# Two graph layers on one core: the turned weights and their product with the attention vectors, made ahead of the neighbour-maximum loop

## The reference, cut to what matters

```
h = relu(layernorm(x))
x = x + max over neighbours j of h[j]              # layer 0
h = relu(layernorm(x))                             # layer 1: graph attention
wh = h @ W
e[i, j] = leaky_relu((wh @ a1)[i] + (wh @ a2)[j], 0.2)
e = where(adj > 0, e, -9e15)
x = x + elu(softmax(e, axis=1) @ wh)
```

## Time and profile before

| | us |
|---|---|
| median of 3 runs | 848.89 (844.92 to 851.26) |
| profiled execution | 848.88 |
| its span, first to last instruction | 847.0 |
| busy: VectorE | 729.1 (86%) |
| busy: TensorE | 722.5 (85%) |
| busy: ScalarE | 480.6 (57%) |
| busy: GpSimd | 347.2 (41%) |
| neighbour loop, first to last ScalarE operation of it | about 19 to 512 |
| from there to the first attention weight on VectorE | 512 to 568.8 |

### The profile page before, as it was taken

How to read it: one execution, slowest core, us unless ns; L and a number is a source line. 1 busy time by engine, 2 the same in 40 slices (tenths; PEclk the granted TensorE clock), 3 DMA queues, 4 the chain that set the end, 5 groups by cost and what they waited for, 6 DMA issues and landing times.

```text
span 847.0 us, 14904 instructions
## 1 busy us (share of the span) xinstructions
PE 722.5 (85%) x5658; PEld 498.5 (59%) x5658; DVE 729.1 (86%) x1121; ACT 480.6 (57%) x594; POOL 347.2 (41%) x320
## 2 busy tenths in 40 slices
PE   1789999999999998999999983247889999999995
PEld 1345444445444444444444442137889999999995
DVE  8899889999999998999999997327479988998994
ACT  3878898888888888888888860134421100110000
POOL 0611055565655655655565666713003321330330
PEclk9999999999999999999999996568899999999998
DMA  9799677987887777877877545202124444444410
GB/s 309 250 363 364 231 250 237 323 258 249 256 259 246 235 240 240 260 250 230 244 243 257 158 144 185 53 13 73 53 100 162 162 150 147 140 149 151 162 63 14
DMA packets 64904, 166.75 MB, mean 197 GB/s; under 512 B 7424, under 2 KB 12160, under 8 KB 60736
## 3 DMA queue, kind: packets, MB, share of 16 engines
q1 hardware_dynamic: 53776, 138.75, 47.2%
q0 software_dynamic: 11056, 27.02, 13.4%
HBM read 121.70 MB, written 44.04 MB: 196 GB/s over the span
## 4 chain that ended last, share of the span: by engine, by line
PE 40%; ACT 27%; issue 16%; DVE 9%; another core or an unknown queue 4%; DMA 2%; POOL 1%; ACTq 0%; DVEq 0%; SPq 0%
PE pick_ps L684 13%; ACT edge_t L344 12%; ACT depth L353 7%; PE order_ps L684 7%; ACT first L352 6%; PE order_ps L519 5%; DVE acc L807 4%; PE key_ps L684 3%; PE flip_ps L684 3%; PE pick_ps L538 3%; DMA subset_max<-keys 1%; PE key_ps L632 1%; DVE rest L1008 1%; PE key_ps L551 1%
## 5 line engine op out<-in xcount | busy, mean ns | idle before, releaser
L316 POOL DMA_INDIRECT found<-subset_max,entry x256 | 273.6, 1069 | 240.0 <-DVE acc L807 109.1
L807 DVE TENSOR_TENSOR acc<-pick_ps,acc 128x1024 f32<-128x1024 f32 x248 | 302.5, 1220 | 26.2 <-PE pick_ps L538 15.6
L1008 DVE SCALAR_TENSOR_TENSOR rest<-depth,acc,stage 128x512 f32<-128x512 f32 x256 | 201.4, 816 | 19.0 <-PE key_ps L684 1.5
L352 ACT ACTIVATE first<-order_ps,neg 128x1024 f16<-128x1024 f32 x128 | 142.6, 1114 | 61.4 <-PE order_ps L519 37.6
L353 ACT ACTIVATE depth<-order_ps,mid 128x1024 f16<-128x1024 f32 x128 | 141.8, 1107 | 0.0
L344 ACT ACTIVATE edge_t<-flip_ps 128x1024 f16<-128x1024 uint16 x128 | 131.2, 1025 | 3.9 <-PE flip_ps L510 2.9
L684 PE MATMUL pick_ps<-keys,rest 128*128 128x129 f32 x1024 | 121.2, 280 | 10.5 <-DVE left L960 6.5
L684 PEld LDWEIGHTS pick_ps<-keys,rest 128*128 128x128 f32 x1024 | 119.6, 197 | 13.3 <-issue 7.4
L519 PE MATMUL order_ps<-edge_t,order_w 128*128 128x512 f16 x256 | 79.5, 393 | 38.5 <-ACT edge_t L344 30.6
L538 PE MATMUL pick_ps<-first,h_hi 128*128 128x512 f16 x256 | 97.6, 381 | 5.1 <-DVE acc L807 5.0
L538 PE MATMUL pick_ps<-second,h_hi 128*128 128x512 f16 x256 | 97.4, 380 | 2.0 <-DVE acc L807 1.1
(11 more groups left out here) (154 smaller groups left out, 818.9 us busy)
## 6 DMA issues: line engine op xcount, KB each, us to landing
stage<-adj SPq DMA_DIRECT2D x64, 1024.0 KB
edge_units<-edge_t SPq DMA_DIRECT2D x64, 512.0 KB
stage<-edge_units SPq DMA_DIRECT2D x32, 1024.0 KB, 4.9
subset_max<-keys POOLq DMA_DIRECT2D x12, 512.0 KB, 8.4
found<-subset_max,entry POOLq DMA_INDIRECT x256
best<-x SPq DMA_DIRECT2D x4, 512.0 KB, 6.3
subset_max<-x POOLq DMA_DIRECT2D x4, 512.0 KB, 8.8
out<-keys POOLq DMA_DIRECT2D x7, 256.0 KB, 2.8
```

Of the source, the lines that this page charges most:

```text
L316: nc.gpsimd.indirect_dma_start(found[:, n % NG, s, :], None, subset_max, bass.IndirectOffsetOnAxis(entry[:, n, s:s + 1], 0)).then_inc(gath ...
L352: nc.scalar.activation(first[:, g % 4, :], order_ps[:, :], ACT.Relu, scale=-1.0, bias=neg[:, :]).then_inc(first_ready, 1)
L807: V.tensor_tensor(acc[:, q % 2, :], pick_ps[k][:, :], acc[:, q % 2, :], ALU.max).then_inc(raised, 1)
L1008: V.scalar_tensor_tensor(out=weight[:, n % WEIGHTS, :], in0=limit[:, q % 2, :], scalar=slope[:, c:c + 1], in1=units[:, m % EDGES, k * TI:( ...
```

## The change

The turned weights, the spread vectors and their product get SBUF tiles of their own (`w_t`, `a_wide`, `wa`) instead of places carved out of `acc`, and are made before the loop. TensorE turns the weights after `rank(0)`, for which it waits for `w_in`, and multiplies after `flip(3)`. ScalarE copies after `select(0)` and after `select(2)`. GpSimd, not VectorE, spreads the vectors, ahead of its low halves. The loop's first use of `key_ps` waits for the second copy. The steps between the loops are taken out.

```diff
+        w_t = sb("w_t", [P, D], F32)
+        a_wide = sb("a_wide", [P, 2 * D], F32)
+        wa = sb("wa", [P, 2 * D], F32)
...
-        w_t, a_wide, wa = carve(D), carve(2 * D), carve(2 * D)
...
 # GpSimd, after the iotas
+                pool.wait_ge(consts_made, 1)
+                pool.wait_ge(w_in, 48)
+                nc.gpsimd.tensor_scalar(a_wide[:, D:2 * D], ones[:, :], a12[:, 0:1], None, ALU.mult).then_inc(wide_made, 1)
+                nc.gpsimd.tensor_scalar(a_wide[:, 0:D], ones[:, :], a12[:, 1:2], None, ALU.mult).then_inc(wide_made, 1)
                 pool.wait_ge(hs_ready, 4)
...
 # ScalarE
                 select(0)
+                act.wait_ge(small_put, 1)
+                nc.scalar.activation(w_t[:, :], wt_ps, ACT.Copy).then_inc(small_took, 1)
                 high(1)
                 edges(2)
                 select(1)
                 edges(3)
                 select(2)
+                act.wait_ge(small_put, 2)
+                nc.scalar.activation(wa[:, :], wa_ps, ACT.Copy).then_inc(small_took, 1)
                 high(2)
...
-                act.wait_ge(small_put, 1)
-                nc.scalar.activation(w_t[:, :], wt_ps, ACT.Copy).then_inc(small_took, 1)
-                act.wait_ge(small_put, 2)
-                nc.scalar.activation(wa[:, :], wa_ps, ACT.Copy).then_inc(small_took, 1)
                 root(0)
...
 # TensorE
                         if n >= 1:
                             pe.wait_ge(keyed, n)
+                        else:
+                            pe.wait_ge(small_took, 2)
...
                 rank(0)
+                pe.wait_ge(w_in, 48)
+                nc.tensor.transpose(wt_ps, w_sb[:, :], ident32[:, :]).then_inc(small_put, 1)
                 flip(2)
                 rank(1)
                 flip(3)
+                pe.wait_ge(small_took, 1)
+                pe.wait_ge(wide_made, 2)
+                nc.tensor.matmul(wa_ps, w_t[:, :], a_wide[:, :], start=True, stop=True).then_inc(small_put, 1)
                 rank(2)
...
                 for g in range(4):
                     rows(g)
-                pe.wait_ge(w_in, 48)
-                nc.tensor.transpose(wt_ps, w_sb[:, :], ident32[:, :]).then_inc(small_put, 1)
-                pe.wait_ge(small_took, 1)
-                pe.wait_ge(wide_made, 2)
-                nc.tensor.matmul(wa_ps, w_t[:, :], a_wide[:, :], start=True, stop=True).then_inc(small_put, 1)
                 for g in range(4, 6):
                     rows(g)
-                pe.wait_ge(small_took, 2)
...
 # VectorE
-                dve.wait_ge(w_in, 48)
-                V.tensor_scalar(a_wide[:, D:2 * D], ones[:, :], a12[:, 0:1], None, ALU.mult).then_inc(wide_made, 1)
-                V.tensor_scalar(a_wide[:, 0:D], ones[:, :], a12[:, 1:2], None, ALU.mult).then_inc(wide_made, 1)
                 dve.wait_ge(x1_in, 16)
```

## The result

The changed kernel took 851.74 us (median of 20 runs, 849.37 to 857.86), the kernel before beside it 849.03 (20 runs, 839.43 to 854.43): 1.0059 of it, interval 1.0034 to 1.0084. It is a little slower, by less than 1%, where 2.5 us of gain were forecast. The profiled execution took 850.31 us (span 848.5) against 848.88, 1.43 more.

What follows compares the result with a forecast made beforehand. ScalarE was taken to pace the neighbour loop, with late signals under GpSimd's gathers making the gaps after it. 848.9 + 2.4 (start) - 4.9 (between the loops) = 846.4 us; range 828 to 854.

Steps and rivals of the forecast that it cites:

- Start, +2.4: Kernel start: waiting for weights and vectors, plus two copies, delays ScalarE and what follows by 2.4 us; bounds 1.7 to 3.6.
- GpSimd's two products, zero: Kernel start: GpSimd's two new 128x128 products, at most 1.57 us each, end before anything needs them and cost zero.
- Root 9.9 sooner: Between the loops: ScalarE's root needs only the moments, so it starts near 530.8 to 530.9, not 540.76, 9.9 us sooner.
- I take the middle mechanism: Between the loops: signals stay about 8 us late per hand-over until about 558.7; gain 4.9 us; chance 43%.
- rival A: Between the loops: columns held until the gathers are over, whenever made, so nothing gained; 851.3 us; chance 20%.
- Rival B: Between the loops: the lateness of signals goes, gaining 22.4 us; 828.9 us; chance 27%.
- Rival C: Between the loops: late signals strike VectorE's six steps, delaying the last gather batch; 857.8 us with two strikes; chance 10%.

Runs made afterwards that it cites:

- after_direct: Changed kernel with the 24 gathers of groups 28 to 30 replaced by plain transfers, so the rows asked for are not fetched: 826.64 us, ratio 1.002.
- before_direct: Kernel before with the 24 gathers of groups 28 to 30 replaced by plain transfers, so the rows asked for are not fetched: 824.85 us, ratio 1.0004.
- after_spaced: Changed kernel, its start too, with a 128x128 GpSimd multiply behind each of the 24 gathers of groups 28 to 30: 829.10 us, ratio 0.9749.
- before_spaced: Kernel before with a 128x128 GpSimd multiply behind each of the 24 gathers of groups 28 to 30: 826.79 us, ratio 0.9722.
- w_first: Changed kernel with the loads of the weights and vectors issued ahead of the first adjacency loads: 847.77 us, ratio 0.9988.
- after_again: Changed kernel, unchanged, timed again beside the kernel before in the third group: 852.54 us, ratio 1.0089.
- root_first: Kernel before with ScalarE's root and first normalisation ahead of the two copies and TensorE's product behind the first columns, start unchanged: 848.97 us, ratio 1.0013.
- w_wait_only: Kernel before with only TensorE's wait for weights and vectors behind its first rank product added at the start: 849.76 us, ratio 1.0038.
- direct_again: Kernel before with the 24 gathers of groups 28 to 30 as plain transfers, run again in the third group: 826.86 us, ratio 0.9804.
- before_pause: Kernel before with GpSimd waiting ahead of the gathers of group 28 until the curve shifts are made: 852.29 us, ratio 1.0065.

## Why the prediction was wrong

**Start, +2.4: right.** ScalarE's h_hi at 23.35 (said 23.30), its second half at 30.80 (30.8), rank(2) at 27.47 (27.45), low halves at 31.94 (32.0), VectorE's wait over at 52.98 (53.2). Of the 2.39 at 32 us, 1.93 arrive at the loop's end (the 514.3 that was said for its last copy is an end; it ended at 513.88). With no hold in either kernel the whole change costs 1.8 us (after_direct less before_direct) and 2.3 (after_spaced less before_spaced). What I didn't look for was that most of the price hangs on the order of SyncE's queue, as w_first showed.

**GpSimd's two products, zero: right.** 1.20 and 0.60 us, over at 24.59, ahead of anything that waits for GpSimd.

**Root 9.9 sooner: nearly.** 533.06 is 7.7 sooner than 540.76; with the 1.93 of the start, 9.6. From root's end to the first normalisation it then took 3.45 us and not 1.30, since three of VectorE's six steps waited 0.5 us each for the step before, and the signal to ScalarE was 0.5 late too; the columns ended 5.5 sooner.

**"I take the middle mechanism", -4.9: this is the step that failed.** It let each signal be late by about 8 us, so that one made 10 us sooner would also arrive sooner, at 544.7. The columns were copied at 560.04 instead, at 560.55 in after_again and at 558.05 in root_first. For these signals the lateness is not a delay that they carry along. It is what is left of the gathers' row when the signal is made: 13.5 us in the kernel before, 20.4 in the changed one, with the same end. That was rival A, to which I gave 20%; its 851.3 is 0.4 off the median. The trace of before had the better evidence for it. Its two signals latest in the row came through 4.3 us after the gathers' end and at their last landing, and I let the two of 7.8 and 2.7 us that did get through outweigh them. I also took the columns' signal for 12.0 us late, by the second group of columns, where the copy needs the first.

Rival A is not the whole rule either. Some late signals get through while the row still runs: the turned weights at 536.25, and VectorE's step at 550.22 in the changed kernel after 6.05 us. w_first's first columns came at 554.37, half a microsecond after the last gather's end. What lets one through and holds the next is not shown.

**Rival B** (lateness goes, 828.9) needs the hold to be away. Then, however, the kernel before has no lateness either, and that was not in my sum: 22.4 us would be gained by both, and the change would still cost its 2.3. In neither of the two conditions seen here does the reordering pay. The Trainium skill, TensorE: Matmul & The Clock Gate, section "The cost: per-tile semaphore tail", gives an increment some 26 ns. The traces leave room for that where gathers are apart (a whole hand-over, from the turn's end to the copy's start, took 0.17 us) and not where they come in a row (a signal up to 20.4 us late).

**Rival C** (VectorE's own steps are struck, the last batch of gathers comes later, slower) did not come about: three steps lost 0.5 us each, and no gap opened in the gathers' row. Its second half can be seen in w_wait_only, where the steps were late because ScalarE's root was, with the other sign: the gathers ran out of buffers, the hold ended sooner and the columns came 6 us early.

**Still open:** what the condition is in which gathers hold signals, which part of the chip holds them, and how it can be told ahead of a run. The traces speak against DMA load (48 GB/s against 273) and code loading (two instruction packets in the 40 us from 520 to 560 of the kernel before). They don't show what a list of indices does that a plain transfer of the same rows doesn't.

## What to carry to other kernels

When a signal is late in a trace, find out whether it is late by a time or until an event, before you move work towards it: look at what ends together with several waits, not at how long each was. Work taken out of a stretch that ends with somebody else's last instruction gains nothing, and what it costs where it is put stays. And look at what the waiting instruction reads: the longest gap of a trace can be an ordinary wait behind another's late signal, as VectorE's 15.6 us were. Here the row of gathers was the thing to change: an instruction of 0.6 us between two of them, on an engine that had time, was worth 23 us, ten times what the change cost.

## What the chip showed that I had not expected

- 24 gathers with index lists, 1.25 us apart behind seven more (31 in a row from 515.23), hold signals of TensorE, and of VectorE to itself (up to 8.8 us, after_again), for up to 20.4 us; those still held at the row's end came 2.5 to 4.7 us after the last gather, one after 0.5. Gathers 1.85 us apart hold none, 1.53 apart next to none, and plain transfers of the same size on the same queue none.
- The first late signal is made 13 to 17 us into the row (528.47 in the kernel before, about 534.2 in the changed one, whose row starts at 517.16). The seven gathers with which the row starts stood bare in before_spaced and direct_again too, and held nothing.
- ScalarE's hand-overs inside the row were prompt: in the kernel before TensorE starts at 536.58 on what ScalarE ended at 536.53, and VectorE at 541.09 on what it ended at 541.05.
- The same kernel took 824.7 us in one group of runs and 844.5 to 849.9 in the others. About all of the difference is this hold, as far as the kernels profiled in that group show; the kernel before itself was profiled only with the hold. A kernel timed in one of the two conditions isn't known in the other.
- In the row, TensorE starts one matmul per 1.40 us although it waits for nothing that the profile names (before_pause, 583 to 591).
- GpSimd's product of 128x128 took 1.20 us the first time and 0.60 the second, 0.55 to 0.6 in most of the 24 later ones.
